# Second layer's experts of a two-layer decoder: low-rank rows stacked, choice weights repeated by DMA

## The reference

```
def _fused_linear(x, W, qa, qb, scale, w):
    out = x @ W.T
    a = jnp.einsum('th,krh->tkr', x, qa)
    b = jnp.einsum('tkr,khr->tkh', a, qb)
    mix = jnp.einsum('tkh,tk->th', b, w)
    return out + scale[None, :] * mix
def expert(muW, gW, gqa, gqb, gs, uW, uqa, uqb, us, dW, dqa, dqb, ds, w):
    xe = x + w @ muW.T
    gate = jax.nn.silu(_fused_linear(xe, gW, gqa, gqb, gs, w))
    up = _fused_linear(xe, uW, uqa, uqb, us, w)
    return _fused_linear(gate * up, dW, dqa, dqb, ds, w)
outs = jax.vmap(expert, ...)(..., soft)
y = jnp.einsum('fth,tf->th', outs, scalar)
```

## Time and profile before

| | us |
|---|---|
| median of 3 runs (1096.1 to 1100.84) | 1097.9 |
| the profiled execution's own time | 1096.5 |
| its span, first to last instruction | 1094.5 |
| block of layer 1's experts, from its first matmul to the end | 215.6 (878.9 to 1094.5) |

### The profile page before, as it was taken

How to read it: one execution, slowest core, us unless ns; L and a number is a source line. 1 busy time by engine, 2 the same in 40 slices (tenths; PEclk the granted TensorE clock), 3 DMA queues, 4 the chain that set the end, 5 groups by cost and what they waited for, 6 DMA issues and landing times. The chain is left out here.

```text
span 1094.5 us, 18969 instructions
## 1 busy us (share of the span) xinstructions
PE 999.0 (91%) x6064; PEld 815.0 (74%) x6064; DVE 717.9 (66%) x2146; ACT 608.3 (56%) x1654; POOL 459.8 (42%) x473
## 2 busy tenths in 40 slices
PE   7999999998996799669899999988878889999996
PEld 5998899887883689537678888965445568777775
DVE  5666766663588456446655767646787557888886
ACT  3656565656222455336576776547874556555553
POOL 5787667761287344366111110210137214444321
PEclk9999999999998899869899999989998989999998
DMA  6732111000011799624301101001003011112101
GB/s 207 257 124 79 30 31 29 16 15 2 1 63 52 253 345 338 212 73 140 95 20 60 33 25 40 1 22 52 2 2 116 1 58 58 58 58 67 50 1 39
DMA packets 83784, 85.61 MB, mean 78 GB/s; under 512 B 8577, under 2 KB 75975, under 8 KB 83568
## 3 DMA queue, kind: packets, MB, share of 16 engines
q1 hardware_dynamic: 79776, 75.59, 21.4%
q0 software_dynamic: 3072, 7.34, 2.2%
q10 hardware_dynamic: 848, 1.57, 0.4%
HBM read 63.36 MB, written 22.02 MB: 78 GB/s over the span
## 5 line engine op out<-in xcount | busy, mean ns | idle before, releaser
L579 POOL TENSOR_TENSOR a_qk<-h,a_by_sin 128x512 f32<-128x512 f32 x64 | 81.9, 1280 | 5.0
L352 DVE CUSTOM_DVE_ANT_0 h<-a_score_ps,mask_bf 128x128 f32<-128x128 f32 (+1 forms) x128 | 40.7, 355 | 64.5 <-PE a_score_ps L345 64.3
L1286 POOL TENSOR_TENSOR a_w_l<-a_w,a_w_h 128x256 fp32r<-128x256 f32 x30 | 21.8, 728 | 115.6 <-ACT a_w_h L1479 115.4
L358 ACT ACTIVATE y_moe<-y_moe,a_nmax 128x128 f32<-128x128 f32 x64 | 25.6, 400 | 75.9 <-DVE a_nmax L352 75.9
L339 DVE COPY a_probsT<-a_turn_ps 128x384 f32<-128x384 f32 x64 | 34.9, 546 | 48.2 <-PE a_turn_ps L269 48.2
L1025 POOL TENSOR_TENSOR e_w_l<-e_w,e_w_h 128x512 fp32r<-128x512 f32 x32 | 40.8, 1276 | 53.1 <-ACT e_w_h L1093 53.1
L80 PE MATMUL a_proj_ps<-a_x_l,a_w_h 128*128 128x512 f32 x128 | 57.2, 447 | 3.6 <-POOL a_w_l L584 3.4
L459 PEld LDWEIGHTS a_proj_ps<-a_w,xT 128*128 128x128 f32 x512 | 59.6, 192 | 0.9 <-issue 0.2
L459 PE MATMUL a_proj_ps<-a_w,xT 128*128 128x128 f32 x512 | 59.8, 275 | 0.0
L755 PE MATMUL t_y_ps<-wo,attnT 128*128 128x256 f32 x256 | 58.7, 383 | 0.0
L2629 POOL TENSOR_TENSOR m_up_l<-m_up_w,m_up_h 128x1024 fp32r<-128x1024 f32 x8 | 19.5, 2434 | 90.1 <-ACT m_up_h L2601 90.1
(11 more groups left out here) (464 smaller groups left out, 3516.2 us busy)
## 6 DMA issues: line engine op xcount, KB each, us to landing
slots<-zeros SPq DMA_DIRECT2D x4, 2048.0 KB, 8.0
e_rows<-slots SPq DMA_DIRECT2D x32, 256.0 KB, 4.7
e_w<-in_L_ffn_w_dram SPq DMA_DIRECT2D x32, 256.0 KB, 4.9
out_slots<-e_out SPq DMA_DIRECT2D x32, 256.0 KB, 4.2
e_w<-in_L_ffn_w_dram SPq DMA_DIRECT2D x32, 128.0 KB, 4.3
...
```

The costliest lines, as they stand in the source:

```text
L352: done = dve.tensor_tensor_reduce(self.probs[:, b, cells], self.score_ps[:, r, cells], self.k.mask_bf[:, cells], -1.0, 3e38, ALU.add, ALU. ...
L358: act.activation(self.probs[:, b, 0:P], self.probs[:, b, 0:P], ACT.Exp, bias=self.nmax[:, b, 0:1], scale=-1.0, accum_out=self.total[:, b, ...
L579: pool.tensor_tensor(qk[:, par, 0 if what == "q" else 1, half * HALF:(half + 1) * HALF], by_cos[:, r, :], by_sin[:, r2, :], ALU.add).then_ ...
```

## The change

- The low-rank rows are stacked. The weighed factors `aw` of a half now go into two tiles of 128 rows: `gate_a` holds the high part of the 64 gate rows over their low part, `up_a` the low part of the 64 up rows over their high part. With weights stacked to match (`lora_g`, `lora_u`: the high part of the rows twice), one plain product does what a pair of half-row products did. `gate_up_lora` has seven plain products in place of six half-row and three plain ones.
- ACT makes `lora_g` and `lora_u` with four copies per expert, and per half a copy for each of `gate_a` and `up_a`. DVE writes the low gate rows (`weigh_rest`), POOL the low up rows (`up_rest`).
- The lower half of the act's second tile: its high and low rows are stacked too, so that `down_input` has five products for six. A copy on ACT then moves the low rows to where `down_out` wants them. Four copies that cleared that tile go.
- The choice weights of experts 1 to 7 are repeated by DMA. ACT keeps the choice weights as plain rows in the route block, SP stores them eight times into DRAM, and two DMAs per half read them back as `wrep`. The product with `rep`, its copy out of PSUM and the loads and cuts of `rep` stay for expert 0 alone.
- On SP these DMAs and the loads of the weights now stand in one row by halves. POOL's `up_rest` stands by experts among its cuts.

```diff
+                        pe.wait_ge(rows_kept, 2)
...
+                    for side in range(2):
+                        act.activation(k.soft_rows[side * SIDE:(side + 1) * SIDE, halves(half)],
+                                       soft_ps[side][0:SIDE, :], ACT.Copy).then_inc(rows_kept, 1)
...
-LOADS1 = 8
+LOADS1 = 7
...
+        if e == 0:
+            sp.dma_start(self.rep_w[:, :], I["rep1"][e]).then_inc(w_in, 16)
...
     def cut_lora_high(self, act, e):
         act.wait_ge(self.lora_scaled, e + 1)
+        tiles = self.lora_s[:, :].rearrange("p (j f) -> p j f", j=GU)
+        for rows in (slice(0, KR), slice(KR, P)):
+            act.activation(self.lora_g[rows, e % 2], tiles[0:KR, 0:GU:2, :], ACT.Copy)
+            act.activation(self.lora_u[rows, e % 2], tiles[KR:P, 1:GU, :], ACT.Copy)
         act.activation(self.lora.h[:, e % 2, :], self.lora_s[:, :], ACT.Copy).then_inc(self.lora_high, 1)
...
             @block.sync
             def _(sp):
-                for e in range(2, F1):
-                    ew.load(sp, e)
+                for r in range(R1):
+                    sp.dma_start(k.soft_dram[:, r, :], k.soft_rows).then_inc(rows_stored, 16)
+                sp.wait_ge(rows_stored, 16 * R1)
+                for n in range(2, N):
+                    e, half = divmod(n, 2)
+                    sp.wait_ge(awd_done, n - 1)
+                    rows = k.soft_dram[e * K1:(e + 1) * K1, :, half * HALF:(half + 1) * HALF].rearrange("j r t -> (j r) t")
+                    for again in range(2):
+                        sp.dma_start(wrep[again * KR:(again + 1) * KR, half, :], rows).then_inc(wrep_in[half], 16)
+                    if half and e + 1 < F1:
+                        ew.load(sp, e + 1)
...
+                def up_rest(n):
+                    pool.wait_ge(aw_high, n + 1)
+                    at_least(pool, gu_done, 2 * n)
+                    pool.tensor_tensor(up_a[0:KR, :], aw[KR:P, :], aw_h[KR:P, :], ALU.subtract).then_inc(up_low, 1)
+                    pool.wait_ge(up_low, n + 1)
...
                 for e in range(1, F1):
+                    if e > 1:
+                        pool.wait_ge(ew.down_low, 2 * e)
+                        up_rest(2 * e - 2)
+                    up_rest(2 * e - 1)
                     ew.scale(pool, e)
...
-                    for left, right in ((lora.h, aw_p.l), (lora.h, aw_p.h), (lora.l, aw_p.h)):
-                        for j in range(2):
-                            rows = slice(j * KR, (j + 1) * KR)
-                            last = pe.matmul(gu_ps[:, j, :], left[rows, e, j * P:(j + 1) * P], right[rows, :],
-                                             start=False, stop=left is lora.l, tile_position=(j * KR, 0))
+                    for j, (left, right) in enumerate(((ew.lora_g, gate_a), (ew.lora_u, up_a))):
+                        pe.matmul(gu_ps[:, j, :], left[:, e, 0, :], right[:, :], start=False, stop=False)
+                        last = pe.matmul(gu_ps[:, j, :], lora.l[:, e, j * P:(j + 1) * P], right[:, :], start=False, stop=True)
...
+                    act.activation(gate_a[0:KR, :], aw[0:KR, :], ACT.Copy)
+                    act.activation(up_a[KR:P, :], aw[KR:P, :], ACT.Copy).then_inc(aw_stacked, 1)
...
+                    act.wait_ge(act_low, 2 * n + 2)
+                    act.activation(act1_p.l[0:KR, n % 2, :], act1_p.h[KR:P, n % 2, :], ACT.Copy
+                                   ).then_inc(rest_kept, 1)
+                    act.wait_ge(rest_kept, n + 1)
...
+                    if n >= 2:
+                        dve.wait_ge(wrep_in[n % 2], 16 * 2 * (n // 2))
+                    at_least(dve, up_low, n)
+                    at_least(dve, aw_stacked, n)
```

More of the change, by code:

```diff
@@ L2550, in __init__ @@
         self.mu = m.sb("m_mu", [P, 2, D], F32R)
-        self.rep = m.sb("m_rep", [P, 2, P], F32R)
+        self.rep = m.sb("m_rep", [P, P], F32R)
+        self.lora_g = m.at("m_lora_g", [P, 2, 2, P], k.wo1_at + 8 * 4 * D, F32R)
+        self.lora_u = m.at("m_lora_u", [P, 2, 2, P], k.wo1_at + 10 * 4 * D, F32R)
         self.w_in = [m.sem("m_w_in0"), m.sem("m_w_in1")]
@@ L2594, in cut_mu_high @@
         self.loaded(act, e)
-        act.activation(self.rep[:, r, :], self.rep_w[:, r, :], ACT.Copy)
+        if e == 0:
+            act.activation(self.rep[:, :], self.rep_w[:, :], ACT.Copy)
         act.activation(self.mu[:, r, :], self.mu_w[:, r, :], ACT.Copy).then_inc(self.mu_high, 1)
@@ L2723, in _ @@
                     ew.cut_down_low(pool, e)
+                pool.wait_ge(ew.down_low, 2 * F1)
+                up_rest(N - 2)
+                up_rest(N - 1)
                 for t in range(0, NT, 2):
@@ L2739, in low_inputs @@
                                   ).then_inc(xe_proj, 1)
-                    pe.matmul(a_ps[:, :], rep[:, e % 2, :], soft, start=True, stop=True
-                              ).then_inc(wrep_proj, 1)
+                    if e == 0:
+                        pe.matmul(a_ps[:, :], rep[:, :], soft, start=True, stop=True).then_inc(wrep_proj, 1)
                 def factors(n):
@@ L2770, in gate_up_lora @@
                     last.then_inc(gu_done, 1)
-                    product(pe, gu_ps[:, 2, :], lora[:, e, 2 * P:3 * P], aw_p[:, :], False, True).then_inc(gu_done, 1)
+                    pe.matmul(gu_ps[:, 2, :], ew.lora_g[:, e, 1, :], gate_a[:, :], start=False, stop=False)
+                    pe.matmul(gu_ps[:, 2, :], ew.lora_u[:, e, 1, :], up_a[:, :], start=False, stop=False)
+                    pe.matmul(gu_ps[:, 2, :], lora.l[:, e, 2 * P:3 * P], aw_h[:, :], start=False, stop=True
+                              ).then_inc(gu_done, 1)
@@ L2773, in down_input @@
                 def down_input(n):
-                    if n == 0:
-                        pe.wait_ge(clear_h, 2)
                     if n % 2 == 0:
                         pe.wait_ge(ew.dqa_low, n // 2 + 1)
-                    for c, a in enumerate((act0_p, act1_p)):
-                        pe.wait_ge(act_low, 2 * n + c + 1)
-                        last = product(pe, xe_ps[:, 0, :], dqa[:, n // 2 % 2, c, :], a[:, n % 2, :], c == 0, c == 1)
-                    last.then_inc(dqa_done, 1)
+                    pe.wait_ge(act_low, 2 * n + 1)
@@ L2783, in down_out @@
+                    product(pe, xe_ps[:, 0, :], dqa[:, n // 2 % 2, 0, :], act0_p[:, n % 2, :], True, False)
+                    pe.wait_ge(act_low, 2 * n + 2)
+                    high, low = dqa[:, n // 2 % 2, 1, :]
+                    pe.matmul(xe_ps[:, 0, :], high, act1_p.h[:, n % 2, :], start=False, stop=False)
+                    pe.matmul(xe_ps[:, 0, :], low, act1_p.h[:, n % 2, :], start=False, stop=True).then_inc(dqa_done, 1)
                 def down_out(n):
@@ L2834, in keep_xe @@
                 def keep_xe(n):
-                    act.wait_ge(wrep_proj, n + 1)
-                    act.activation(wrep[:, n % 2, :], a_ps[:, :], ACT.Copy).then_inc(wrep_kept, 1)
+                    if n < 2:
+                        act.wait_ge(wrep_proj, n + 1)
+                        act.activation(wrep[:, n % 2, :], a_ps[:, :], ACT.Copy).then_inc(wrep_kept, 1)
                     for c in range(DC):
@@ L2842, in keep_aw @@
                     act.wait_ge(aw_done, n + 1)
-                    act.activation(aw_p.h[:, :], aw[:, :], ACT.Copy).then_inc(aw_high, 1)
+                    act.activation(aw_h[:, :], aw[:, :], ACT.Copy).then_inc(aw_high, 1)
+                    act.activation(gate_a[0:KR, :], aw[0:KR, :], ACT.Copy)
+                    act.activation(up_a[KR:P, :], aw[KR:P, :], ACT.Copy).then_inc(aw_stacked, 1)
                 keep_xe(0)
@@ L2847, in _ @@
                 keep_xe(1)
-                act.wait_ge(cleared, 1)
-                for r in range(2):
-                    act.activation(act1_p.h[KR:P, r, :], act1[KR:P, :], ACT.Copy)
-                    act.activation(act1_p.l[KR:P, r, :], act1[KR:P, :], ACT.Copy).then_inc(clear_h, 1)
                 for n in range(N):
@@ L2899, in weigh_rest @@
                     dve.wait_ge(aw_high, n + 1)
-                    dve.tensor_tensor(aw_p.l[:, :], aw[:, :], aw_p.h[:, :], ALU.subtract).then_inc(aw_low, 1)
+                    dve.tensor_tensor(gate_a[KR:P, :], aw[0:KR, :], aw_h[0:KR, :], ALU.subtract).then_inc(gate_low, 1)
                 def add(n, q):
```

34 lines of the change are left out of this document (24 added, 10 removed).

## The result

The changed kernel takes 1156.6 us (median of four runs, 1155.5 to 1158.6), the kernel before beside it 1097.1. The ratio is 1.054 (95% interval 1.051 to 1.057): slower by 5.4%. The profiled execution has a span of 1154.8 us, 60.3 more than before.

A forecast was written before the change was run, and what follows sets the result against it. TensorE and the ACT and DVE chain were taken as nearly tied, so delays on ACT, POOL or SP come through. 1096.5 + 19.8 (A) + 28.7 (B) + 1.1 (route) + 7.0 (clock) - 1.2 = 1151.9, said as 1152; range 1129 to 1171.

The forecast's parts named there:

- A, six stretches: Stretch ending at an even half's down-factor weighing product: 3.3 us longer from late loads, experts 2 to 7, 19.8 in all.
- B, seven stretches: Stretch beginning at that product's end in an even half: 4.1 us longer, experts 1 to 7, 28.7 in all.
- clock: TensorE's granted clock falls to some 0.8 a round behind its empty places, costing 1.0 us per round, 7 in all.
- route block: The same four lora copies on ACT delay the softmax's exp there by 1.1 us.
- last two halves: No weights to fetch or cut, so TensorE ends last and saved products count: 2 x 0.6 = 1.2 us gained.
- Loads: On SP the next expert's loads stand behind the choice-weight copies, so ACT's m_mu starts 4.4 us late in odd halves.
- slack of 1.1: In A, the half's three waits for TensorE (0.24, 0.17, 0.67 us) absorb 1.1 us of the loads' delay.
- POOL's order: up_rest ahead of the next expert's cuts: low_inputs at T + 4.8 (T: even half's down-factor product ends), m_up_h 2.85 us late.
- Lora copies: Four more copies on ACT in front of the silu in B, 0.31 us each, 1.24 a round.
- The three other copies of a half: New ACT copies, 0.61 us each, said to end before m_xe is there, hidden while ACT waits for low_inputs.
- One wait only: Rival: the loads arrive in time, so A's 19.8 us drop out and the time is 1132; chance 0.08.
- TensorE alone: Rival: both waits are covered and TensorE alone decides, 0.6 us gained per half, time 1087; chance 0.03.

The follow-up runs named there:

- the run with fillers: The changed kernel with products whose result is overwritten in TensorE's two empty places of a round, both waits kept; 1150.8 us, ratio 1.048.
- the run with late loads: The kernel before with one wait added on SP, so an expert's loads wait for the same product as in the changed kernel; 1115.5 us, ratio 1.015.
- the run with early loads: The changed kernel with the next expert's seven loads moved on SP half a round sooner, behind the even half's weight copies; 1132.6 us, ratio 1.031.
- The run with both moves and the lora copies out of the way: The changed kernel with loads half a round sooner, up_rest behind mu's low part, and ACT's lora copies in its wait ahead of aw_h; 1103.7 us, ratio 1.008.

## Why the prediction was right, point by point

The forecast was 1152 and the range 1129 to 1171; the time is 1156.6. The terms, measured from the stretches, with the clock's share taken from the run with fillers:

| term | forecast | measured |
|---|---|---|
| A, six stretches | 19.8 | 20.4 (24.4 less 4.0 of clock) |
| B, seven stretches | 28.7 | 33.5 (35.8 less 2.3 of clock) |
| clock | 7 | 6.4 at least |
| route block | 1.1 | 1.1 at the exp, 0.3 by the end of half 0 |
| last two halves | -1.2 | -0.6 |

- **Loads.** The step held, and the numbers of the round shown too: the loads are complete 8.8 us after L2997 (forecast 8.83), and m_mu is 4.3 late for 4.4. That they meet so well is partly luck. Eight issues took 4.24 us (951.01 to 955.25) for 3.83, and the landing 4.5 for 5.0; and this round has the earliest m_mu of the six. Over all six it is 4.9 late on average (4.3 to 5.8). A grew by 0.7 to 1.0 less than that, the clock's cost included; in the run with late loads, where the clock stayed at 1.00, by 1.0 to 1.1 less, which bears out the slack of 1.1. That run shows the step in the kernel before, and the run with early loads takes it away. The copies' own wait was nothing, as assumed: nothing waits for a landing of `m_wrep`.
- **POOL's order.** Low_inputs at T + 4.47 for T + 4.8 (4.3 to 5.0 in the seven rounds), and the cut of the up weights at T + 7.17 for T + 7.1. The parts were off and cancelled, so the match is partly luck: up_rest took 1.29, not 1.74, because POOL was ahead and DVE paid (1.71; so in six rounds of seven), lora_s took 1.33 for 1.01, down_s 0.72 for 1.20 and mu 0.99 for 0.75.
- **Lora copies.** The mis-sized term. I took 0.31 each from copies of 128x256; the 64x256 copies start 0.41 to 0.43 apart. 1.70 a round in place of 1.24 is 3.2 us over seven rounds, most of what B has over the forecast. Most of the rest lies in expert 1, whose stretch grew by 6.4 where the others grew by 4.9 on average: before, it was 0.9 shorter than they, and after it is as long.
- **The three other copies of a half** were called hidden behind low_inputs. With POOL's wait in place they were. The run with both moves and the lora copies out of the way has no such cover, and keeps 7.1 us over the kernel before; its rows put most of that down to these copies.
- **Clock.** The fall came where it was forecast, behind each empty place. It went to 0.90 to 0.92 in A, in B to 0.80 to 0.82 in four stretches and 0.88 or 0.89 in three; I had said some 0.8 for a whole round. Its price was about right: 6.4 at least, for 7.
- **Last two halves.** The rep product was counted in them, but halves 14 and 15 have no low_inputs left to run. What they save is 0.1 + 0.23 each, 0.7 in both; 0.6 was measured. The seven plain products take 1.64 us from the first to the first down product (954.62 to 956.26), for 1.6 forecast and 1.70 before.
- **Rivals.** One wait only (1132) did not come with the change itself: both waits are there. The run with early loads, which leaves POOL's wait alone, takes 1132.6; that this is so close to the rival's 1132 is partly luck, as both the forecast (1152 for 1156.6) and A's share (19.8 for 24 to 26) were low. TensorE alone (1087) did not come even with both waits gone, since ACT's copies were next in line.
- **Row tiles.** By the Trainium skill's table (TensorEngine Tiling (Array Packing), "Theoretical Speedup") the plain products would have been 0.23 a half dearer; they were 0.06 cheaper, so the trace stands against the full factor of two for these pairs.
